# Adding expert results onto the token rows: VectorE sums against accumulating GpSimd transfers

## The chip, the cores and the metric

The kernel runs on one core of a Trainium2 chip. The metric is device time in microseconds. The kernel before takes 485.4 us (median of three runs, 483.75 to 485.8). The profiled execution shown below took 485.2 us, and its span from the first to the last instruction is 483.5 us, so 1.7 us lie outside the span. Times in the rows count from the start of the span.

## What is computed

4096 tokens of width 256 go through a cross-attention block and then through a mixture of eight experts, of which each token uses two.

```python
x = x + cross_attention(layernorm(x), ctx)        # called x1 below
h = layernorm(x)
probs = softmax(h @ gate_w.T); topw, sel = top_k(probs, 2); topw /= topw.sum(-1)
expert_out[e] = (silu(g) * u) @ w2[e].T           # g, u = split(h @ w1[e].T)
out = x + sum over the two chosen experts of topw * expert_out[e]
```

The last line is what the change is about: for each token, two result rows of 256 floats are added to that token's row of x1, and the sum is the output.

## The kernel before

The tokens are 32 tiles of 128 rows. The first part (some 310 us) does the attention tile by tile and keeps x1 for all tiles in SBUF, in the tensor `x1` (printed as `x` in the trace). Each tile's normalised rows are scattered into a table in memory that is sorted by expert.

The second part is a software pipeline over 71 slots of 128 sorted rows. A turn i of `turn2` does a piece of four slots on each engine: SyncE (SP) has loaded slot i, TensorE transposes slot i, multiplies slot i-1 with the first weights, transposes the activations of slot i-2 and multiplies slot i-3 with the second weights. ScalarE (ACT) in turn i does, in this order, `hst_hi(i)`, `silu(i-1)`, `au_hi(i-2)` and `y_copy(i-3)`; VectorE (DVE) does `hst_lo(i)`, `gate_mult(i-1)` and `au_lo(i-2)`. GpSimd (POOL) sends each finished slot with `send_y(slot)`, an indirect transfer that scatters 128 rows of 1 KB into `expert_out`, where a token's two results lie side by side. The slot's result buffer is one of four (`YRING`), so `y_copy(m)` waits for the send of slot m-4. Note the lag: `send_y(s)` follows `y_copy(s)`, and that is part of turn s+3.

Because the first 16 tiles are routed ahead of the rest, their results are complete when slot `DONE` = 39 has been sent; 24, 28, 30 and 32 tiles are complete after 55, 63, 67 and 71 slots.

What is done with the results before the change: for each pair of tiles g (16 of them), SP loads 512 KB of `expert_out` into one of five SBUF buffers (`load_results`), DVE adds the two choices (`add_choices`, line 1320) and then x1 (`add_rows`, line 1325), and ACT issues the store of the pair (`store_results`, line 821). These steps are written into the turns: from turn 48 (`FIN_FIRST`) on, DVE does `add_choices` in one turn and `add_rows` in the next, and ACT issues the store a turn later.

Each engine runs its own instructions strictly in the order in which they are written; a wait stops all that follows it on that engine. The lines that the steps touch:

Of the kernel before, what the change touches and what calls it, by code (L numbers as in the profile page):

```python
# [7 lines left out]
ALU = mybir.AluOpType  # L8
ACT = mybir.ActivationFunctionType
AX = mybir.AxisListType  # L10
F32 = mybir.dt.float32
# [6 lines left out]
P = 128  # L18
B, L, D = 64, 64, 256
# [5 lines left out]
NT = T // P  # L25
# [11 lines left out]
NSLOT = 71  # L37
BOUNDS = (16, 24, 28, 30)
EARLY = BOUNDS[0]
# [55 lines left out]
def build_in(nc, stack, x, ctx_t, w_proj, w_out, w_exp, w_gate, bias, norm_q, norm_k, out,  # L95
             sorted_rows, expert_out):
    def sb(name, shape, dt):
        return stack.enter_context(nc.sbuf_tensor(name, shape, dt))

    def sem(name):  # L100
        return stack.enter_context(nc.semaphore(name))
# [47 lines left out]
    v_bd = sb("v_bd", [P, 2, NB, 2, NPAIR * VW], F32)  # L149

    qp = sb("qp", [P, 2, NQ, 2, KC, NB, L], F16)
# [21 lines left out]
    row = sb("row", [P, 2, SKEW, ROW], F32)  # L173
# [27 lines left out]
    def words(t, pattern):  # L201
        return t.rearrange(pattern)
# [35 lines left out]
    cum2_of = words(square[:, :, :], "p a d -> p (a d)").bitcast(F32)[:, 0:NE * NE].rearrange("p (e f) -> p e f", e=NE)  # L238
    past2_of = past2_of.rearrange("p (a s) -> p a s", a=2)

    def fin_buffers(t, n):
        return [t[:, at * 4 * D:(at + 1) * 4 * D].rearrange("p (m k d) -> p m k d", k=2, m=2) for at in range(n)]

    fin_early = [b for t, n in (
        (words(row[:, :, :, :], "p k s d -> p (k s d)"), 2),
        (qp[:, :, :, :, :, :, :].rearrange("p u g n c b l -> p (u g n c b l)").bitcast(F32), 2),
        (words(v_bd[:, :, :, :, :], "p u b q d -> p (u b q d)"), 1)) for b in fin_buffers(t, n)]
    FIN_BUF = len(fin_early)
    FIN_EARLY = BOUNDS[1] // 2
    FIN_LATE = BOUNDS[-1] // 2  # L250
    assert EARLY_DONE + EARLY >= DONE[1]
    fin_late = [we[:, n * 4 * D:(n + 1) * 4 * D].bitcast(F32).rearrange("p (m k d) -> p m k d", k=2, m=2)
                for we in (we_h, we_l) for n in range(NT // 4)]
    fin_in = (fin_early * 3)[0:FIN_LATE] + fin_late[0:NT // 2 - FIN_LATE]
    FIN_FIRST = EARLY_DONE + 9

    gate_cols = slice(D, DG)
    count_cols = slice(D, D + 3 * NE)
# [43 lines left out]
    y_sent = [sem(f"y_sent{r}") for r in range(4)]  # L302
    names2 = """h2_transposed h2_h_ready h2_l_ready gate_up silu_ready act_ready act_transposed
        au_h_ready au_l_ready y_done y_ready""".split()
    F = {n: sem(n) for n in names2}
    fin_loaded = [sem(f"fin_loaded{n}") for n in range(8)]
    fin_stored = [sem(f"fin_stored{n}") for n in range(FIN_BUF)]
    fin_sum1, fin_sum2 = sem("fin_sum1"), sem("fin_sum2")


    tr_bank = bank[:, 0, :]
# [24 lines left out]
    def _(sp):  # L336
# [97 lines left out]
            load_slot(slot)  # L434
        send_pads()

        ev = expert_out.rearrange("(p t k) d -> p t k d", k=2, p=P)

        def load_results(g):
            if FIN_BUF <= g < FIN_LATE:  # L440
                sp.wait_ge(fin_stored[g % FIN_BUF], 16 * (g // FIN_BUF))
            need(sp, fin_loaded[g % 8], 16 * (g // 8))
            sp.dma_start(fin_in[g], ev[:, 2 * g:2 * g + 2, :, :]).then_inc(fin_loaded[g % 8], 16)

        for slot in range(RING, NSLOT):
            if slot == FULL:
                sp.wait_ge(plan, PLAN)
                sp.wait_ge(pads_sent, 16 * (NE + 1))
                for s in range(SKEW):
                    for k in range(2):  # L450
                        sp.wait_ge(row_sent[k][s], 16 * (NT // SKEW))

            sp.wait_ge(y_sent[slot % YRING], ((slot - RING) // YRING + 1) * 16)
            load_slot(slot)
            g = (slot - EARLY_DONE - RING) // 2
            if (slot - EARLY_DONE - RING) % 2 == 0 and 0 <= g < FIN_EARLY:
                load_results(g)
        for g in range((NSLOT - 1 - EARLY_DONE - RING) // 2 + 1, FIN_EARLY):
            load_results(g)
        for done, low, high in zip(DONE[2:], BOUNDS[1:], BOUNDS[2:] + (NT,)):  # L460
            for r in range(4):
                sp.wait_ge(y_sent[r], 16 * ((done - 1 - r) // YRING + 1))
            for g in range(low // 2, high // 2):
                load_results(g)
        for n in range(FIN_BUF):
            sp.wait_ge(fin_stored[n], 16 * ((NT // 2 - 1 - n) // FIN_BUF + 1))


    @block.gpsimd
    def _(pool):  # L470
        done = [0]
# [147 lines left out]
        for slot in range(NSLOT):  # L619
            send_y(slot // RING, slot % RING)  # L620


    @block.scalar
    def _(act):
# [132 lines left out]
        t = Tile(0, 0)  # L757
# [58 lines left out]

        ov = out.rearrange("(t p) d -> p t d", p=P)

        def store_results(g):
            act.wait_ge(fin_sum2, g + 1)  # L820
            act.dma_start(ov[:, 2 * g:2 * g + 2, :], fin_in[g][:, :, 0, :]).then_inc(fin_stored[g % FIN_BUF], 16)

        for i in range(NSLOT + 3):
            turn2(i // RING, i % RING, True)
            g = (i - FIN_FIRST - 2) // 2
            if (i - FIN_FIRST) % 2 == 0 and 0 <= g < FIN_EARLY:
                store_results(g)
        for g in range((NSLOT - FIN_FIRST) // 2 + 1, NT // 2):
            store_results(g)


    @block.vector
    def _(dve):
        done = [0]
# [325 lines left out]
        for n in range(2):  # L1160
            t = Tile(0, n)
# [153 lines left out]
            if i == 8 + CLASSES:  # L1315
                list_shared()

        def add_choices(g):
            dve.wait_ge(fin_loaded[g % 8], 16 * (g // 8 + 1))
            dve.tensor_tensor(fin_in[g][:, :, 0, :], fin_in[g][:, :, 0, :], fin_in[g][:, :, 1, :], ALU.add  # L1320
                              ).then_inc(fin_sum1, 1)

        def add_rows(g):
            dve.wait_ge(fin_sum1, g + 1)
            dve.tensor_tensor(fin_in[g][:, :, 0, :], fin_in[g][:, :, 0, :], x1[:, 2 * g:2 * g + 2, :], ALU.add
                              ).then_inc(fin_sum2, 1)

        for i in range(NSLOT + 3):
            turn2(i // RING, i % RING, True)
            g = (i - FIN_FIRST) // 2  # L1330
            if 0 <= g < FIN_EARLY:
                if (i - FIN_FIRST) % 2 == 0:
                    add_choices(g)
                else:
                    add_rows(g)
        for g in range(NT // 2):
            if FIN_FIRST + 2 * g > NSLOT + 2 or g >= FIN_EARLY:
                add_choices(g)
            if FIN_FIRST + 2 * g + 1 > NSLOT + 2 or g >= FIN_EARLY:
                add_rows(g)  # L1340


    @block.tensor
# [377 lines left out]
```

## Time and profile before

| what | value |
|---|---|
| median of three runs | 485.4 us |
| profiled execution, and its span | 485.2 us, 483.5 us |
| PE busy, of the span | 438.5 us (91%) |
| DVE busy | 388.1 us (80%) |
| ACT busy | 276.5 us (57%) |
| POOL busy | 308.7 us (64%) |
| TensorE clock granted, mean | 0.984 |

A busy time is an average over parts with different limits: PE is busy for 99% of the turns in the middle of the second part and for 92% of its last 22 turns, where DVE has the extra sums. So the part and its waits are read by stretches. A clock of 1.00 is 2.4 GHz, 0.50 is 1.2 GHz.

### The profile page before, as it was taken

Reading aid. Unit: us, or ns where it says so; the run is one execution under the profiler, and the core shown is the slowest. Engines: PE = TensorE matmul, PEld = TensorE weight load, DVE = VectorE, ACT = ScalarE, POOL = GpSimd, SP = SyncE. Lnnn points to the kernel's source line nnn. Section 1 sums busy time; section 2 is a strip of 40 time slices with the busy share of each in tenths; the row PEclk is TensorE's granted clock in tenths of the full one; section 3 lists DMA queues with packets and bytes.
Section 4 is the critical chain, followed back from the end, with each engine's and each line's share of the span. In section 5 each row is a group of like instructions: output and inputs, shape, how many; then the busy total and the mean of one; then the engine's idle time right before and its main releaser. Section 6 shows DMA issues by size and latency. Waiting matters only on the chain.

```text
span 483.5 us, 15249 instructions
## 1 busy us (share of the span) xinstructions
PE 438.5 (91%) x4428; PEld 383.3 (79%) x4428; DVE 388.1 (80%) x1336; ACT 276.5 (57%) x802; POOL 308.7 (64%) x529
## 2 busy tenths in 40 slices
PE   7898999999999999889999998889999999998980
PEld 3567888878887887778888886679999999898870
DVE  7544888888888898898998978778876767899893
ACT  5353667666665666656666653365566656655650
POOL 6842547887888878777788786576444444444451
PEclk9997999999999999999999999999999999999996
DMA  7253443233232332423333322545444445789964
GB/s 206 82 142 82 140 141 111 87 108 95 81 114 85 104 94 86 118 75 94 104 93 92 105 86 75 148 162 166 133 132 123 127 128 153 240 254 316 309 201 157
DMA packets 55514, 64.62 MB, mean 134 GB/s; under 512 B 9599, under 2 KB 49034, under 8 KB 55434
## 3 DMA queue, kind: packets, MB, share of 16 engines
q1 hardware_dynamic: 44602, 42.59, 31.9%
q0 software_dynamic: 6480, 16.85, 9.8%
q10 hardware_dynamic: 4352, 4.20, 2.5%
q8 instruction: 39, 0.64, 0.6%
q14 instruction: 41, 0.34, 0.2%
HBM read 32.73 MB, written 23.14 MB: 116 GB/s over the span
## 4 chain that ended last, share of the span: by engine, by line
PE 48%; POOL 24%; issue 13%; DVE 12%; ACT 1%; DMA 1%; POOLq 1%; DVEq 0%; ACTq 0%; SPq 0%
PE bank L1351 9%; PE bank L1352 8%; PE bank L1353 8%; POOL sorted_rows L542 7%; PE bank L1592 4%; POOL r_qk L498 3%; POOL we_l L490 3%; POOL ct_l L484 2%; POOL rstd L498 2%; PE bank L1412 2%; PE bank L1625 2%; PE bank L1624 2%; PE bank L1614 2%; PE bank L1613 2%; POOL row L527 1%
## 5 line engine op out<-in xcount | busy, mean ns | idle before, releaser
L614 POOL DMA_INDIRECT expert_out<-probs,late x71 | 72.7, 1024 | 75.1 <-ACT probs L800 70.3
L542 POOL DMA_INDIRECT sorted_rows<-row,place_i x64 | 69.0, 1079 | 33.4 <-POOL row L534 14.8
L1351 PE MATMUL bank<-we_h,xt_h 128*128 x142 | 51.7, 364 | 0.8 <-DVE xt_l L1265 0.8
L705 ACT ACTIVATE probs<-bank 128x1024 f32<-128x1024 f32 x32 | 32.8, 1026 | 23.4 <-PE bank L1465 21.5
L1352 PE MATMUL bank<-we_l,xt_h 128*128 x142 | 45.8, 323 | 0.0
L1353 PE MATMUL bank<-we_h,xt_l 128*128 x142 | 45.7, 322 | 0.0
L788 ACT ACTIVATE xn<-bank 128x176 f32<-128x176 f32 x71 | 22.6, 318 | 37.4 <-PE bank L1353 37.3
L1275 DVE SCALAR_TENSOR_TENSOR probs<-xn,late,bank 128x128 f32<-128x128 f32 x71 | 24.5, 345 | 20.9 <-ACT xn L788 20.2
L932 DVE TENSOR_REDUCE bank<-bank 128x16 f32<-128x1024 f32 x32 | 39.1, 1223 | 2.0 <-PE bank L1400 2.0
L498 POOL TENSOR_TENSOR rstd<-veps,half_neg 128x1 f32<-128x1 f32 x64 | 36.6, 572 | 5.3
L800 ACT COPY probs<-bank 128x256 f32<-128x256 f32 x71 | 26.4, 372 | 18.7 <-PE bank L1625 17.2
L1412 PE MATMUL bank<-v_bd,probs 128*64 128x34 f32 x1024 | 35.3, 225 | 0.2 <-ACT probs L705 0.2
L1465 PE MATMUL bank<-neg_max_t,head_of 128*128 128x128 bf16 x256 | 35.2, 219 | 0.0
L1461 PE MATMUL bank<-qp,late 128*128 128x256 f16 x128 | 34.9, 273 | 0.0
L1463 PE MATMUL bank<-qp,late 128*128 128x256 f16 x128 | 34.9, 273 | 0.0
L1462 PE MATMUL bank<-qp,late 128*128 128x256 f16 x128 | 34.9, 273 | 0.0
L1265 DVE TENSOR_TENSOR xt_l<-bank,xt_h 128x256 fp32r<-128x256 f32 x71 | 30.1, 424 | 5.8 <-ACT xt_h L782 2.5
L1592 PE MATMUL bank<-ident,late 128*128 128x128 f32 x142 | 29.4, 289 | 5.8 <-issue 5.2
L670 ACT COPY neg_max_t<-bank 128x128 bf16<-128x128 bf16 x32 | 8.5, 265 | 45.4 <-PE bank L1441 45.4
L1412 PEld LDWEIGHTS bank<-v_bd,probs 128*64 128x64 f32 x1024 | 33.4, 141 | 0.4 <-ACT probs L705 0.4
L782 ACT CAST xt_h<-bank 128x256 fp32r<-128x256 f32 x71 | 26.6, 375 | 9.6 <-PE bank L1592 7.6
L1359 PE MATMUL bank<-bias_hl,ones_row 128*128 128x264 f32 (+1 forms) x96 | 31.0, 323 | 0.0
(234 smaller groups left out, 1597.0 us busy)
## 6 DMA issues: line engine op xcount, KB each, us to landing
late<-sorted_rows SPq DMA_DIRECT2D x71, 129.0 KB, 2.4
we_f<-w_exp SPq DMA_DIRECT2D x32, 152.0 KB
v_bd<-v_sb SPq DMA_DIRECT2D x128, 34.0 KB
ctx_in<-ctx_t SPq DMA_DIRECT2D x32, 128.0 KB, 2.4
qp<-q_hl SPq DMA_DIRECT2D x128, 32.0 KB
x<-x SPq DMA_DIRECT2D x3, 1024.0 KB, 5.7
row<-expert_out SPq DMA_DIRECT2D x6, 512.0 KB, 5.1
qp<-expert_out SPq DMA_DIRECT2D x6, 512.0 KB, 4.4
```

The costliest lines, as they stand in the source:

```text
L498: pool.tensor_tensor(out_, tmp, half_neg[:, 0:tmp.shape[1]], ALU.pow).then_inc(done_, 1)
L542: pool.indirect_dma_start(sorted_rows, bass.IndirectOffsetOnAxis(ap=place_i[:, t.slot // 2, k, t.par:t.par + 1], axis=0), row[:, k, t.slot ...
L614: pool.indirect_dma_start(expert_out, bass.IndirectOffsetOnAxis(ap=hs(r)[:, D:D + 1].bitcast(U32), axis=0), y_sb[:, r % YRING, :], None, b ...
L932: dve.tensor_reduce(row_max, score_bank.rearrange("p (h k) -> p h k", h=NH), AX.X, ALU.max).then_inc(S["max_found"], 1)
L1351: pe.matmul(dst, a_h, b_h, start=start, stop=False)
L1352: pe.matmul(dst, a_h, b_l, start=False, stop=False)
L1353: return pe.matmul(dst, a_l, b_h, start=False, stop=stop)
L1412: ins = pe.matmul(av_bank[b * L:(b + 1) * L, g * 2 * VW:(g + 1) * 2 * VW], probs[:, t.par, at:at + L], v_bd[:, t.par, b, :, g * VW:(g + 1) ...
L1461: pe.matmul(dst, k_h, q_h, start=True, stop=False)
L1462: pe.matmul(dst, k_h, q_l, start=False, stop=False)
L1465: ins = pe.matmul(dst[:, gh * P:(gh + 1) * P], head_of[:, (b * KC + c) * NQ // 2 + gh, :], neg_max_t[:, t.par, :], start=False, stop=gh == ...
L1592: ins = pe.transpose(bank[:, p, c * P:(c + 1) * P], hs(r)[:, c * P:(c + 1) * P], ident[:, :])
```

## The change

Results of tiles 0 to 29 are no longer loaded, summed by DVE and stored from a buffer. Instead POOL issues transfers that add rows of `expert_out` onto `x1` in SBUF (`accum_op=ALU.add`), for four tiles at a time (a fold), one transfer for the first choice (k = 0) and one for the second (k = 1). The fold's k = 1 waits for the landing of its k = 0. There are seven folds of four tiles and one of two tiles, 16 transfers in all. ACT stores each fold from `x1` (512 KB) when both have landed. Only the last two tiles are loaded by SP and summed by DVE as before, and their store goes out last.

```diff
-    fin_early = [...]            # five SBUF buffers; FIN_EARLY, FIN_FIRST, fin_late and so on go
+    FOLDS = [(low, min(low + 4, high), done) for low, high, done in zip((0,) + BOUNDS, BOUNDS, DONE)
+             for low in range(low, high, 4)]
+    free = 0
+    for f, (low, high, done) in enumerate(FOLDS):
+        at = max(free, done + 2)
+        ADDS.setdefault(at, []).append((f, 0))
+        ADDS.setdefault(at + 2, []).append((f, 1))
+        STORES.setdefault(min(at + 6, NSLOT + 2), []).append(f)
+        free = at + 1
...
+    def results_done(eng, done):
+        for r in range(YRING):
+            eng.wait_ge(y_sent[r], 16 * ((done - 1 - r) // YRING + 1))
...
-            if (slot - EARLY_DONE - RING) % 2 == 0 and 0 <= g < FIN_EARLY:
-                load_results(g)          # SP; and the later loads of the same kind
+        results_done(sp, NSLOT)
+        sp.dma_start(fin_in, ev[:, LAST_TILES, :, :]).then_inc(fin_loaded, 16)
+        sp.wait_ge(fin_stored, 16 * (len(FOLDS) + 1))
...
+        def add_results(f, k):           # POOL
+            low, high, done = FOLDS[f]
+            if k == 0:
+                results_done(pool, done)
+            else:
+                pool.wait_ge(fold_added[f], 16)
+            pool.dma_start(x1[:, low:high, :], ev[:, low:high, k, :], accum_op=ALU.add).then_inc(fold_added[f], 16)
+        for slot in range(NSLOT + 3):
+            if slot < NSLOT:
+                send_y(slot // RING, slot % RING)
+            for f, k in ADDS.get(slot, ()):
+                add_results(f, k)
...
-            act.wait_ge(fin_sum2, g + 1) # ACT, a pair of tiles
+        def store_results(f):            # ACT, a fold
+            low, high, done = FOLDS[f]
+            act.wait_ge(fold_added[f], 32)
+            act.dma_start(ov[:, low:high, :], x1[:, low:high, :]).then_inc(fin_stored, 16)
         for i in range(NSLOT + 3):
             turn2(i // RING, i % RING, True)
+            for f in STORES.get(i, ()):
+                store_results(f)
+        act.wait_ge(fin_sum2, 1)
+        act.dma_start(ov[:, LAST_TILES, :], fin_in[:, :, 0, :]).then_inc(fin_stored, 16)
...
-                    add_choices(g)       # DVE, inside the turns: 16 pairs
-                    add_rows(g)
+        dve.wait_ge(fin_loaded, 16)      # DVE, after the last turn: one pair
+        dve.tensor_tensor(fin_in[:, :, 0, :], fin_in[:, :, 0, :], fin_in[:, :, 1, :], ALU.add).then_inc(fin_sum1, 1)
+        dve.wait_ge(fin_sum1, 1)
+        dve.tensor_tensor(fin_in[:, :, 0, :], fin_in[:, :, 0, :], x1[:, LAST_TILES, :], ALU.add).then_inc(fin_sum2, 1)
```

The schedule that these rules give: the transfers of fold f stand on POOL behind `send_y` of the slots 41, 42, 43, 44 (k = 0) and 43, 44, 45, 46 (k = 1) for folds 0 to 3; 57, 58 and 59, 60 for folds 4 and 5; 65 and 67 for fold 6; 69 and 71 for fold 7. The stores stand on ACT at the end of turns 47, 48, 49, 50, then 63, 64, 71 and 73.

POOL before, the end of its program: the last scatter transfers of the first part, then the sends of all slots in one run (`expert_out<-probs`; each row gives the operation and what it waits for).

```order
L529 TENSOR_TENSOR row<-e_gap,row 128x2 [waits weight_set2]
L534 COPY row<-result_row 128x2 [waits row2_ready]
L542 DMA sorted_rows<-row,place_i 33920x258 [waits weight_set3,place_set,ids_set] x2
L534 COPY row<-result_row 128x2 [waits row2_ready]
L542 DMA sorted_rows<-row,place_i 33920x258 [waits weight_set3,place_set,ids_set] x2
L614 DMA expert_out<-probs,late 8192x256 [waits y_ready] x71
L90 UNCONDITIONAL_BRANCH
```

Nothing stood between two sends.

POOL now, from the sends of slots 0 to 41 on (`x<-expert_out` is a fold's transfer onto x1; line numbers are those of the changed kernel).

```order
L602 DMA expert_out<-probs,late 8192x256 [waits y_ready] x42
L614 DMA x<-expert_out 128x4x256 [waits y_sent2,y_sent3,y_sent1,y_sent0]
L602 DMA expert_out<-probs,late 8192x256 [waits y_ready]
L614 DMA x<-expert_out 128x4x256 [waits y_sent2,y_sent3,y_sent1,y_sent0]
L602 DMA expert_out<-probs,late 8192x256 [waits y_ready]
L614 DMA x<-expert_out 128x4x256 [waits fold_added0]
L614 DMA x<-expert_out 128x4x256 [waits y_sent2,y_sent3,y_sent1,y_sent0]
L602 DMA expert_out<-probs,late 8192x256 [waits y_ready]
L614 DMA x<-expert_out 128x4x256 [waits fold_added1]
```

Between the sends stand now the transfers that add; the one that waits for `fold_added0` (fold 0, k = 1) comes two sends behind that fold's first, and the sends of slots 44 and later stand behind it.

ACT before, around the first store: the four operations of turns 50 and 51 and the store of the first pair of tiles.

```order
L788 ACTIVATE xn<-bank 128x176 [waits act_ready,gate_up]
L793 CAST at_h<-bank 128x256 [waits y_done,act_transposed]
L800 COPY probs<-bank 128x256 [waits y_sent3,y_done]
L821 DMA out<-row 128x2x256 [waits fin_sum2]
L782 CAST xt_h<-bank 128x256 [waits gate_up,h2_transposed]
L788 ACTIVATE xn<-bank 128x176 [waits act_ready,gate_up]
```

This store, the first of 16, has moved three turns ahead and carries four tiles.

ACT now, turns 47 and 48 with the stores of folds 0 and 1 (L801 is `y_copy`, of slots 44 and 45 here).

```order
L794 CAST at_h<-bank 128x256 [waits y_done,act_transposed]
L801 COPY probs<-bank 128x256 [waits y_sent0,y_done]
L823 DMA out<-x 128x4x256 [waits fold_added0]
L783 CAST xt_h<-bank 128x256 [waits gate_up,h2_transposed]
L789 ACTIVATE xn<-bank 128x176 [waits act_ready,gate_up]
L794 CAST at_h<-bank 128x256 [waits y_done,act_transposed]
L801 COPY probs<-bank 128x256 [waits y_sent1,y_done]
L823 DMA out<-x 128x4x256 [waits fold_added1]
```

A store waited for a sum of DVE (`fin_sum2`) and waits now for both transfers of its fold (`fold_added`); behind it stands, as before, the next turn's `hst_hi`.

## Rows read from the trace of the kernel before

**Rows 1.** Busy time by engine over the span, from the page
```profile
PE 438.5 (91%) x4428; PEld 383.3 (79%) x4428; DVE 388.1 (80%) x1336; ACT 276.5 (57%) x802; POOL 308.7 (64%) x529
```

**Rows 2.** Busy time in stretches: turns 14 to 47, turns 48 to 69, the rest
```profile
core 0: us, PE busy (x) PEld busy (x) DVE busy (x) ACT busy (x) POOL busy (x), PEclk, DMA share, GB/s
344.12:414.40 70.28, 69.83 (x510) 67.26 (x509) 50.71 (x170) 42.98 (x136) 32.75 (x34) 1.00 0.45 132
414.40:465.44 51.04, 47.08 (x331) 43.68 (x331) 46.86 (x133) 29.44 (x88) 24.78 (x23) 1.00 0.88 284
465.44:483.50 18.06, 5.25 (x36) 4.36 (x34) 9.89 (x21) 3.04 (x9) 5.17 (x5) 0.76 0.49 152
```

**Rows 3.** Timeline of DVE, one turn with a sum: start, us, engine, line, operation
```profile
442.33 0.42 DVE L1265 TENSOR_TENSOR xt_l<-bank,xt_h 128x256 fp32r<-128x256 f32 x1
...
443.77 0.69 DVE L1320 TENSOR_TENSOR row<-row 128x512 f32<-128x512 f32 x1
444.50 0.42 DVE L1265 TENSOR_TENSOR xt_l<-bank,xt_h 128x256 fp32r<-128x256 f32 x1
```

**Rows 4.** Chain that ended last, its end: start us, us, what
```profile
467.46 0.69 DVE row L1320
...
473.22 2.63 DMA expert_out<-probs,late
475.98 3.46 DMA we_h<-expert_out
479.46 0.70 DVE we_h L1320
480.19 0.69 DVE we_h L1325
```

**Rows 5.** Timeline of ACT: y_copy of slots 43 and 44
```profile
411.61 0.37 ACT L800 COPY probs<-bank 128x256 f32<-128x256 f32 x1 [0.22 <-PE bank L1625]
...
413.72 0.37 ACT L800 COPY probs<-bank 128x256 f32<-128x256 f32 x1 [0.22 <-PE bank L1625]
```

**Rows 6.** Timeline of POOL: the sends of slots 41, 42 and 43
```profile
408.69 0.97 POOL L614 DMA_INDIRECT expert_out<-probs,late  x1 [1.03 <-ACT probs L800]
410.76 0.97 POOL L614 DMA_INDIRECT expert_out<-probs,late  x1 [1.10 <-ACT probs L800]
412.75 0.97 POOL L614 DMA_INDIRECT expert_out<-probs,late  x1 [1.02 <-ACT probs L800]
```

**Rows 7.** Timeline of DVE and PE: hst_lo of slot 45, and what uses it
```profile
408.23 0.42 DVE L1265 TENSOR_TENSOR xt_l<-bank,xt_h 128x256 fp32r<-128x256 f32 x1
...
409.55 0.41 PE L1351 MATMUL bank<-we_h,xt_h 128*128 x1
```

**Rows 8.** Line 443, SP's loads of 512 KB of results: issue, us to landing
```profile
L443 SPq DMA_DIRECT2D row<-expert_out x6: 332/436/458, 408.2 to 452.6; - x6
...
DMA to landing us min/median/max: 3.5/4.6/6.8
```

**Rows 9.** Line 821, ACT's stores of 256 KB: us to landing
```profile
DMA to landing us min/median/max: 2.1/3.9/6.8
```

**Rows 10.** POOL's own DMA queue: packets, MB, share of 16 engines' span
```profile
q0 software_dynamic: 6480, 16.85, 9.8%
```

**Rows 11.** Timeline of PE around an idle time in the first part
```profile
35.72 0.38 PE L1368 MATMUL bank<-ident,xn 128*128 128x128 f32 x2
38.41 1.06 PE L1400 MATMUL bank<-late,qp 128*64 128x128 f16 x16 [2.32 <-issue]
```

**Rows 12.** Busy time by microsecond there; the eighth number is the clock
```profile
36.00:37.00 1.00, 0.10 (x1) 0.00 (x0) 0.47 (x1) 1.00 (x3) 0.70 (x1) 1.00 1.09 307
37.00:38.00 1.00, 0.00 (x0) 0.00 (x0) 0.56 (x2) 0.27 (x1) 0.00 (x0) 0.93 0.70 205
...
43.00:44.00 1.00, 1.00 (x4) 0.81 (x3) 0.47 (x2) 0.00 (x0) 0.00 (x0) 0.50 0.09 26
44.00:45.00 1.00, 1.00 (x6) 0.48 (x6) 0.00 (x0) 0.12 (x1) 0.00 (x0) 0.66 0.15 40
```

More of the change, by code:

```diff
@@ L239, in build_in @@
     past2_of = past2_of.rearrange("p (a s) -> p a s", a=2)
[L241 to L255, printed above, removed]
+    FOLDS = [(low, min(low + 4, high), done) for low, high, done in zip((0,) + BOUNDS, BOUNDS, DONE)
+             for low in range(low, high, 4)]
+    LAST_TILES = slice(BOUNDS[-1], NT)
+    fin_in = words(row[:, :, :, :], "p k s d -> p (k s d)")[:, 0:4 * D].rearrange("p (m k d) -> p m k d", k=2, m=2)
+    assert NT - BOUNDS[-1] == 2
+    ADDS = {}
+    STORES = {}
+    free = 0
[5 more added lines that the diff above has]
+        free = at + 1
     gate_cols = slice(D, DG)
@@ L305, in build_in @@
     F = {n: sem(n) for n in names2}
-    fin_loaded = [sem(f"fin_loaded{n}") for n in range(8)]
-    fin_stored = [sem(f"fin_stored{n}") for n in range(FIN_BUF)]
+    fold_added = [sem(f"fold_added{f}") for f in range(len(FOLDS))]
+    fin_loaded, fin_stored = sem("fin_loaded"), sem("fin_stored")
     fin_sum1, fin_sum2 = sem("fin_sum1"), sem("fin_sum2")
+    ev = expert_out.rearrange("(p t k) d -> p t k d", k=2, p=P)
+    def results_done(eng, done):
+        for r in range(YRING):
+            eng.wait_ge(y_sent[r], 16 * ((done - 1 - r) // YRING + 1))
     tr_bank = bank[:, 0, :]
@@ L435, in _ @@
         send_pads()
[L437 to L443, printed above, removed]
         for slot in range(RING, NSLOT):
@@ L454, in _ @@
             load_slot(slot)
-            g = (slot - EARLY_DONE - RING) // 2
-            if (slot - EARLY_DONE - RING) % 2 == 0 and 0 <= g < FIN_EARLY:
-                load_results(g)
[L458 to L466, printed above, removed]
+        results_done(sp, NSLOT)
+        sp.dma_start(fin_in, ev[:, LAST_TILES, :, :]).then_inc(fin_loaded, 16)
+        sp.wait_ge(fin_stored, 16 * (len(FOLDS) + 1))
     @block.gpsimd
@@ L617, in send_y @@
             ).then_inc(y_sent[r % YRING], 16)
-        for slot in range(NSLOT):
-            send_y(slot // RING, slot % RING)
+        def add_results(f, k):
[10 more added lines that the diff above has]
+                add_results(f, k)
+        assert max(ADDS) < NSLOT + 3
     @block.scalar
@@ L1316, in turn2 @@
                 list_shared()
[L1318 to L1326, printed above, removed]
         for i in range(NSLOT + 3):
             turn2(i // RING, i % RING, True)
-            g = (i - FIN_FIRST) // 2
-            if 0 <= g < FIN_EARLY:
-                if (i - FIN_FIRST) % 2 == 0:
-                    add_choices(g)
-                else:
-                    add_rows(g)
[L1336 to L1340, printed above, removed]
+        dve.wait_ge(fin_loaded, 16)
+        dve.tensor_tensor(fin_in[:, :, 0, :], fin_in[:, :, 0, :], fin_in[:, :, 1, :], ALU.add).then_inc(fin_sum1, 1)
+        dve.wait_ge(fin_sum1, 1)
+        dve.tensor_tensor(fin_in[:, :, 0, :], fin_in[:, :, 0, :], x1[:, LAST_TILES, :], ALU.add).then_inc(fin_sum2, 1)
     @block.tensor
```

7 lines of the change are left out of this document (removed).

## The prediction

> **What bounds the kernel now.** I read the busy times first, then the stretches of the second part, then timelines of single turns, then the end of the chain. PE is busy for 91% of the span [rows 1], and in the turns without sums it sets the pace: turns 14 to 47 take 70.28 us, of which PE works 69.83, so a turn is 70.28 / 34 = 2.07 us; DVE needs 50.71 / 34 = 1.49 us of it [rows 2]. From turn 48 on, DVE does a sum of 0.69 us in each turn: 1.49 + 0.69 = 2.18, and a turn with a sum starts 2.17 us after the one before it [rows 3]. DVE is the limit there: 51.04 us for 22 turns, 46.86 of them DVE's [rows 2]. After the last send the chain is serial: landing 2.63 us, load 3.46, two sums 0.70 and 0.69, and then the last store to the end of the span, 483.5 - 480.9 = 2.6 us [rows 4].
>
> **What is removed.** With no sums, turns 48 to 69 fall back to PE's pace: 51.04 - 22 x 2.07 = 5.5 us. One more sum stands on the chain in the tail, 0.69 us [rows 4]. Together -6.2 us. SP's 15 loads and ACT's smaller stores are off the chain and I count them at nothing; the same bytes move in the new transfers.
>
> **What is added: a wait on ACT.** The point is the order. Fold 0's k = 1 stands on POOL behind the send of slot 43. Its store stands on ACT at the end of turn 47, and turn 47 ends with the copy of slot 44, because a copy is three turns behind its slot's number. In today's times: the copy of slot 43 ends at 411.61 + 0.37 = 411.98 [rows 5]; the send starts 0.77 later and takes 0.97, so POOL is free at 413.72 [rows 6]; ACT ends the copy of slot 44 at 414.09 [rows 5]. So ACT waits for a transfer that starts at most 0.37 us before. All of turn 48 on ACT is queued behind it: `hst_hi(48)`, which PE's first multiplication of slot 48 needs. PE has slack: `hst_lo` ends at 408.65 and the multiplication that needs it starts at 409.55 [rows 7], 0.9 us.
>
> **The price of a transfer, L, from its start on POOL to its landing.** No row shows an accumulating transfer, so bounds. Below: the last send, 128 rows, lands after 2.63 us [rows 4]; a plain load of the same 512 KB needs 3.5 at the fastest [rows 8]. Above: a fold has 512 rows of 1 KB, a send 128; if POOL's 0.97 us [rows 6] grew with the rows it were 3.9 us, and with the median plain load behind it L = 3.9 + 4.6 = 8.5. I take the nearest row: the median plain load of 4.6 us [rows 8], with POOL's 0.97 for issuing in place of SP's 0.44 [rows 8]: L = 5.1.
>
> The rule that speaks for a short L: the Trainium skill, "DMA: Bandwidth & Descriptors", section "Anatomy of one DMA — SWDGE (gpsimd) path", says that generating descriptors is a small part of a transfer and that many can be emitted before it shows. No row here has two sizes of POOL transfer, so the trace neither confirms nor denies it; by it POOL's share would stay near 0.97, which is the value taken: 506 us in the sum below, against 545 with the 3.9.
>
> **The sum with L = 5.1.** Fold 0's k = 0 starts behind the send of slot 41, at 408.69 + 0.97 = 409.66 [rows 6], and lands at 414.76; its k = 1 waits for that and lands at 419.86. ACT stands from 414.09 to 419.86, 5.8 us. Then ACT needs about 1.7 us for its issue and the turn's four operations, whose inputs are ready. Followed on in this way (POOL: 0.97 for each transfer and each send, in the order of its program), the stores are released at 419.9, 422.8, 428.3 and 431.3; without waits the fourth would be due at 414.09 + 3 x 2.06 = 420.3. That is 11.0 us, less PE's slack of 0.9: **10.1 us** for folds 0 to 3. Folds 4 and 5 are the same as 0 and 1, and POOL has less to do between them: 5.8 + 0.2 - 0.9 = **5.1 us**. Fold 6's store stands on ACT between the copies of slots 68 and 69, another 5.8 us on the way to the last send; there fold 7's k = 0 also stands on POOL before the last send (0.97 us). With some of it running beside the short last turns, the end comes **5.3 us** later; fold 7's own two transfers and store end at about the same time as the last pair's.
>
> **The clock.** After its matmul of 35.72 PE does nothing until 38.41 [rows 11]. The granted clock falls from 1.00 (2.4 GHz) at the end of this idle time and is 0.50 (1.2 GHz) until some 44.3 [rows 12], 6.5 us, while PE is at work from 38.41 on. Half of 6.5 us is lost: 3.2 us. The stops of folds 0 and 4 (and 2) leave PE idle for longer than those 2.3 us. Part of the slow time falls into the smaller waits that follow, so I count one drop for each of the two groups of folds: **6.4 us**. In the tail little PE work is left.
>
> Sum: -6.2 + 10.1 + 5.1 + 5.3 + 6.4 = +20.7. Against the profiled execution's own 485.2 us that is 505.9: **506 us**. The profiled execution is 0.2 below the median of 485.4, so no correction.
>
> **Ends.** The same walk with L = 3.5 gives 5.9 + 2.2 + 2.7 and between no and two clock drops: 490 to 496. With L = 2.63 it is 4.1 + 1.4 + 1.9 and no drop (PE stands 1.4 us): 486. With L = 8.5, 3.9 of it on POOL, the sends stand behind the descriptors too: 29.2 + 15.8 + 14.3 + 6.4 - 6.2 = +59.5: 545.
>
> **Rivals.**
>
> *Two reads for each row.* An adding transfer reads the row in memory and the row of x1, so the 16 engines might need twice the time for it. POOL's queue moved 16.85 MB in 9.8% of 16 x 483.5 us [rows 10], 45 us of one engine for each MB; another 0.52 MB over 16 engines is 1.5 us. L = 6.6 gives 14.7 + 7.9 + 8.3 + 6.4 - 6.2 = +31: 516 us. For it: the engines are busy for 0.88 of turns 48 to 69 already [rows 2], so the extra work cannot hide. Against it: the waits themselves thin out the other traffic. The Trainium skill states such a rule for collectives ("Collectives: The Full Stack", section "The bandwidth ceiling: the fold count and why AG ≠ RS ≠ AR"): a reduction runs at about half the rate of a gather because it reads two sources for each chunk. No run here shows it yet.
>
> *POOL becomes the bound.* If descriptors cost by the row, eight transfers of 3.9 us and six sends stand in six turns; time 525 to 545. Against it: a part of the send's 0.97 is surely fixed.
>
> *The transfer is quick.* L of 2.6 to 3.9 gives 486 to 498.
>
> *The other side: faster.* The stores' wait is hidden, as it is now. Then the sums' 6.2 us come back, less about 1 us for fold 7's transfer before the last send: 480 us. It needs the second transfer to land within 0.37 + 0.9 = 1.3 us of its start; above that each fold's store costs PE time, and at L of about 2.5 the gain is used up. The shortest landing of any result transfer is 2.1 us, a plain 256 KB store at the end, beside nothing else [rows 9].
>
> **Chances.** Forecast (500 to 511): 0.43. Two reads (511 to 525): 0.25. POOL the bound: 0.12. Quick: 0.15, of which 0.05 within 0.5% of before. Faster: 0.05. Half a per cent, 2.4 us, is about what a measurement of this kernel can tell from no change. So faster 0.05, same 0.05, slower 0.90. The range reaches from the quick case's 490 to 528, just into the case of POOL; what is left out is most of that case, the faster one and the quickest transfers, 0.2 together.
>
> **What the profile will show.** Right: ACT's longest waits are the stores of folds 0, 2, 4 and 6, about 5 to 6 us each, released by the adding transfers; PE idle beside them, granted clock 0.50 behind the stops; DVE turns without a sum at 1.5 us of work; POOL rows of about 1 us for 512 rows. Wrong: adding rows of 3 us and more on POOL (the case of POOL); landings above 6 us behind short POOL rows (two reads); no wait of ACT at the stores, with turns of 2.07 us to the end (faster). If ACT's waits are there but PE's turns do not stretch, the slack of 0.9 us was read too small.

## The result, and the profile after

The changed kernel takes 522.6 us (median of four runs, 521.9 to 522.8) against 484.8 us for the kernel before in the same session (four runs, 483.8 to 485.8): ratio 1.0785, 95% interval 1.0761 to 1.0808. It is 37.9 us slower; the forecast was about 21 us slower, 506 us, with a range of 490 to 528. The profiled execution took 522.4 us, its span is 520.6 us. Lines of the kernel after differ from those before by a few: `y_copy` is L801, `hst_hi` L783, `hst_lo` L1266, `send_y` L602, the adding transfers L614, a fold's store L823.

The page's busy times [rows 1] say that PE works 7 us longer for the same 4428 multiplications, and DVE 20 us less.

```profile
PE 445.6 (86%) x4428; PEld 390.5 (75%) x4428; DVE 368.1 (71%) x1306; ACT 274.9 (53%) x802; POOL 328.3 (63%) x545
```

By stretches (columns as in [rows 2]): turns 14 to 47, the first group of folds, quiet turns, the second group, and the rest.

```profile
343.29:411.55 68.26, 67.80 (x495) 65.11 (x493) 49.21 (x165) 41.88 (x132) 33.17 (x34) 1.00 0.43 125
411.55:453.00 41.45, 26.10 (x142) 23.49 (x142) 13.49 (x46) 11.17 (x38) 19.08 (x18) 0.75 0.99 215
453.00:465.21 12.21, 11.87 (x86) 11.19 (x85) 8.54 (x29) 7.60 (x24) 6.90 (x7) 1.00 0.45 132
465.21:492.69 27.48, 19.40 (x122) 18.32 (x121) 11.76 (x41) 10.04 (x32) 12.94 (x13) 0.81 0.74 156
492.69:520.60 27.91, 5.84 (x36) 4.88 (x34) 4.53 (x13) 2.94 (x9) 10.02 (x9) 0.66 0.57 115
```

Up to 411.55 nothing has changed. In the first group PE works for 26 of 41 us while the 16 DMA engines are busy for 0.99 of the time; in the quiet turns between the groups PE is again at work all the time.

Who holds PE is in the waits of ACT from 405 us on (engine, line waited at, releaser: us in all, times, longest):

```profile
ACT xt_h L783 <- DMA x<-expert_out: 34.2, 5, 9.3
...
ACT at_h L794 <- DMA x<-expert_out: 8.6, 1, 8.6
```

The six waits are the stores of folds 0, 1, 2, 4, 5 and 6 (the profile books a wait for a store at the next operation, `hst_hi`, and at `au_hi` in the tail). They are 42.8 us in all, and PE stands beside them: in the two groups DVE waits for ACT's `hst_hi`, and PE for DVE.

```profile
DVE xt_l L1266 <- ACT xt_h L783: 37.7, 12, 9.5
...
PE bank L1335 <- DVE xt_l L1266: 19.0, 4, 6.9
```

How much of the loss hangs on the place of these waits, and how much on the transfers, is for the experiments. One of the waits in ACT's timeline (start, us, operation, idle ahead of it), against [rows 5]: the copy of slot 44, the store, and the next turn's first operation.

```profile
412.88 0.37 ACT L801 COPY probs<-bank 128x256 f32<-128x256 f32 x1 [0.23 <-PE bank L1609]
422.02 0.42 ACTq L823 DMA_DIRECT2D out<-x  x1
422.54 0.37 ACT L783 CAST xt_h<-bank 128x256 fp32r<-128x256 f32 x1 [9.29 <-DMA x<-expert_out]
```

The transfers themselves, L614 on POOL: ns of one (min/median/max), and from issue to landing.

```profile
L614 POOL DMA_DIRECT2D x<-expert_out x16: 1242/1388/1885, 408.9 to 512.2; - x16
...
DMA to landing us min/median/max: 4.6/6.8/13.2
```

So POOL needs 1.39 us for 512 rows where a send of 128 took 0.97 [rows 6], and the landing is 6.8 us in the median where the plain loads of 512 KB had 4.6 [rows 8]. (Fold 7's two transfers are of 256 KB, and the 4.6 is one of them.) POOL's timeline in the first group shows the transfers one behind the other:

```profile
415.31 2.67 POOL L614 DMA_DIRECT2D x<-expert_out  x2 [0.80 <-DMA expert_out<-probs,late]
...
425.54 1.35 POOL L614 DMA_DIRECT2D x<-expert_out  x1
...
433.59 1.30 POOL L614 DMA_DIRECT2D x<-expert_out  x1 [1.15 <-DMA x<-expert_out]
```

The first `x2` is fold 0's second transfer and fold 2's first; the next send starts behind both.

What the clock did beside it, in stretches of 2 us (the eighth number), with PE's busy time and the DMA share:

```profile
416.00:418.00 2.00, 1.00 (x6) 0.81 (x7) 0.00 (x0) 0.00 (x0) 1.98 (x2) 1.00 1.21 232
418.00:420.00 2.00, 0.29 (x2) 0.05 (x1) 0.00 (x0) 0.00 (x0) 1.72 (x2) 0.97 1.18 205
420.00:422.00 2.00, 0.00 (x0) 0.00 (x0) 0.00 (x0) 0.00 (x0) 2.00 (x2) 0.50 1.21 224
...
430.00:432.00 2.00, 1.60 (x5) 1.61 (x6) 1.24 (x5) 0.56 (x3) 0.64 (x1) 0.50 1.20 245
432.00:434.00 2.00, 2.00 (x11) 1.77 (x10) 0.00 (x0) 0.00 (x0) 0.85 (x2) 0.62 1.17 246
434.00:436.00 2.00, 0.07 (x1) 0.00 (x0) 0.00 (x0) 0.00 (x0) 0.90 (x1) 1.00 1.17 238
436.00:438.00 2.00, 0.00 (x0) 0.00 (x0) 0.00 (x0) 0.00 (x0) 0.00 (x0) 0.73 1.16 286
```

The clock falls to 0.50 (1.2 GHz) once PE has stood, as in [rows 12], and stays there until 433; when PE stands again, at 434, it falls a second time in the same group. A DMA share above 1 means that the records of packets overlap, so a share counts the time that packets take, and what they wait for may be in it. In these windows the engines move 205 to 286 GB/s, over the whole first group 215; before, turns 48 to 69 had a share of 0.88 and 284 GB/s [rows 2]. More of the packets' time, and less moved: that is new.

The chain's end, against [rows 4]: fold 6's second transfer, its store on ACT, the last copies, and then the same serial end as before with a 0.61 us piece of fold 7's transfer ahead of the last send.

```profile
498.29 6.03 DMA x<-expert_out
504.34 0.38 ACTq L823
...
507.25 0.61 POOL x L614
507.87 1.04 issue
508.90 3.04 DMA expert_out<-probs,late
512.09 3.57 DMA row<-expert_out
```

Where the 37 us of span are, from the starts of `hst_lo` on DVE (the experiments below are in the same table; times in us):

| kernel | turns 47 to 56 | 57 to 62 | 63 to 69 | turn 70 to the end |
|---|---|---|---|---|
| before | 22.9 | 14.2 | 16.0 | 18.1 |
| after | 42.7 | 13.0 | 25.4 | 27.9 |
| late stores | 32.7 | 13.4 | 17.3 | 25.7 |
| plain copies | 37.6 | 13.0 | 21.0 | 22.0 |
| both | 25.5 | 13.4 | 14.5 | 22.7 |
| 4 KB stretches | 43.4 | 12.9 | 24.5 | 27.9 |
| late, 4 KB, spread | 25.4 | 16.0 | 17.6 | 24.2 |

After less before: +19.8, -1.2, +9.4 and +9.8, and the first part ended 0.8 us earlier; together +37.

### The profile page after: what moved, and what is told of

It reads as the page before. It is cut to its first block, busy times and chain, and to the rows that moved or that the text cites. A ratio compares the mean times of both kernels' runs of the same rounds, so it can differ in the third digit from the quotient of the medians.

```text
span 520.6 us, 15216 instructions
## 1 busy us (share of the span) xinstructions
PE 445.6 (86%) x4428; PEld 390.5 (75%) x4428; DVE 368.1 (71%) x1306; ACT 274.9 (53%) x802; POOL 328.3 (63%) x545
## 4 chain that ended last, share of the span: by engine, by line
PE 39%; POOL 25%; issue 14%; DVE 10%; DMA 9%; ACT 2%; POOLq 1%; ACTq 0%; DVEq 0%; SPq 0%
PE bank L1335 8%; PE bank L1336 7%; PE bank L1337 7%; POOL sorted_rows L530 7%; DMA x<-expert_out 6%; POOL r_qk L486 3%; PE bank L1576 3%; POOL we_l L478 3%; POOL ct_l L472 2%; POOL rstd L486 2%; DMA expert_out<-probs,late 2%; POOL expert_out L602 2%; PE bank L1396 1%; POOL row L515 1%; PE bank L1609 1%
## 5 line engine op out<-in xcount | busy, mean ns | idle before, releaser
L602 POOL DMA_INDIRECT expert_out<-probs,late x71 | 70.4, 992 | 88.0 <-ACT probs L801 79.8
L1335 PE MATMUL bank<-we_h,xt_h 128*128 x142 | 54.5, 384 | 19.9 <-DVE xt_l L1266 19.9
L1266 DVE TENSOR_TENSOR xt_l<-bank,xt_h 128x256 fp32r<-128x256 f32 x71 | 30.1, 425 | 43.5 <-ACT xt_h L783 40.3
L783 ACT CAST xt_h<-bank 128x256 fp32r<-128x256 f32 x71 | 26.6, 375 | 40.5 <-DMA x<-expert_out 34.2
L1336 PE MATMUL bank<-we_l,xt_h 128*128 x142 | 47.9, 337 | 0.0
L1337 PE MATMUL bank<-we_h,xt_l 128*128 x142 | 47.8, 336 | 0.0
L1335 PEld LDWEIGHTS bank<-we_h,xt_h 128*128 128x128 f32 x142 | 28.5, 201 | 21.7 <-issue 21.7
L1276 DVE SCALAR_TENSOR_TENSOR probs<-xn,late,bank 128x128 f32<-128x128 f32 x71 | 24.6, 346 | 28.0 <-ACT xn L789 27.9
L789 ACT ACTIVATE xn<-bank 128x176 f32<-128x176 f32 x71 | 22.6, 318 | 37.9 <-PE bank L1337 37.3
L801 ACT COPY probs<-bank 128x256 f32<-128x256 f32 x71 | 26.6, 374 | 17.6 <-PE bank L1609 17.5
L1335 PE MATMUL bank<-we_h,at_h 128*128 x71 | 27.2, 383 | 10.0 <-DVE at_h L1289 8.7
L1576 PE MATMUL bank<-ident,late 128*128 128x128 f32 x142 | 30.3, 296 | 4.9 <-issue 4.7
```

What stands on the lines that cost most here:

```text
L602: pool.indirect_dma_start(expert_out, bass.IndirectOffsetOnAxis(ap=hs(r)[:, D:D + 1].bitcast(U32), axis=0), y_sb[:, r % YRING, :], None, b ...
L1335: pe.matmul(dst, a_h, b_h, start=start, stop=False)
L1336: pe.matmul(dst, a_h, b_l, start=False, stop=False)
L1337: return pe.matmul(dst, a_l, b_h, start=False, stop=stop)
L1576: ins = pe.transpose(bank[:, p, c * P:(c + 1) * P], hs(r)[:, c * P:(c + 1) * P], ident[:, :])
```

## The experiments

Two theories. The first: what costs is where the store's wait stands, on ACT in front of the next turn. The second: what costs is the transfer, because the addition makes the DMA engines do each byte twice. Both had their part in the forecast; the runs were to say how much each has, and whether the forecast's other terms hold.

**Stores six turns later.**

```diff
-        STORES.setdefault(min(at + 6, NSLOT + 2), []).append(f)
+        STORES.setdefault(min(at + 12, NSLOT + 2), []).append(f)
```

> The changed kernel, with each fold's store put six turns later on ScalarE (12 turns behind the fold's first transfer, not 6). Nothing is left out. Theory 1 (the place of the wait costs the time: ScalarE stands at the store, and its next turn with it): nearly all of the loss of the two groups of folds goes, PE stays at some 2.06 us a turn, and the time is about 482 us (before's 484.8, less 5.5 for the sums in turns 48 to 69, plus some 3 in the tail). Theory 2 (the 16 DMA engines are full: an adding transfer needs some 2.3 times the engine time of a send, and eight of them in a row, 4.2 MB, fill all 16 engines for some 27 us, during which the loads of the slots, the sends and the waits on GpSimd stand too): the wait only moves from ScalarE to GpSimd's queue and to the slots' data, the first group of folds still costs some 10 us, and the time is about 495 to 500 us. Under both, the landings stay as in the changed kernel (median near 6.8 us), longest near 12 us.

Measured: 501.2 us, ratio to before 1.0347 (1.0296 to 1.0399). 21.4 us of the 37.9 went, not all. ACT no longer waits for the adds. POOL does, with the sends behind it, and PE's longest waits stand now ahead of the first transposition of a turn (L1576). The waits from 400 to 480 us, and the stretch from turn 40 to the end:

```profile
PEld bank L1576 <- issue: 12.4, 16, 1.8
POOL x L614 <- DMA x<-expert_out: 10.6, 4, 4.3
```

```profile
395.36:498.80 103.44, 71.28 (x486) 65.47 (x484) 49.06 (x163) 41.78 (x129) 57.19 (x51) 0.90 0.85 192
```

The time is just above the 495 to 500 us of the second theory. The landings stay, as both said (6.9 us in the median, 12.1 the longest).

**Plain copies in place of the addition.**

```diff
-            pool.dma_start(x1[:, low:high, :], ev[:, low:high, k, :], accum_op=ALU.add).then_inc(fold_added[f], 16)
+            pool.dma_start(x1[:, low:high, :], ev[:, low:high, k, :]).then_inc(fold_added[f], 16)
```

> The changed kernel, with plain copies in place of the adding transfers: same bytes, same rows, same waits and queue, without the accumulation (the sum of the result rows is left out). Theory 2 (an adding transfer moves each row twice through the DMA engines): the engine time of GpSimd's queue for the eight folds falls from some 105 us for each MB to some 45, landings fall from a median of 6.8 us to 4.6 to 5.1, and the time to about 506 us, what the forecast's sum gives with a transfer of 5.1 us. Rival (512 rows of 1 KB from GpSimd's queue are slow as such, and the accumulation is free): landings stay near 6.8 us and the time near 522 us.

Measured: 504.9 us, ratio 1.0414 (1.0353 to 1.0474). The transfers of this kernel (L614), and the stretch from turn 40 to the end:

```profile
L614 POOL DMA_DIRECT2D x<-expert_out x16: 755/808/851, 407.7 to 495.9; - x16
...
DMA to landing us min/median/max: 3.1/5.2/8.4
```

```profile
396.11:503.90 107.79, 74.84 (x486) 70.55 (x484) 48.78 (x163) 40.74 (x129) 47.26 (x51) 0.84 0.58 184
```

The same stretch of before and of after:

```profile
398.08:483.50 85.42, 68.65 (x486) 63.99 (x484) 68.68 (x193) 42.54 (x129) 37.72 (x35) 0.95 0.73 232
```

```profile
397.28:520.60 123.32, 77.48 (x486) 71.80 (x484) 48.75 (x163) 40.57 (x129) 57.13 (x51) 0.80 0.72 161
```

Time by DMA share is the work of all 16 engines: 85.42 x 0.73 = 62.4 us before, 107.79 x 0.58 = 62.5 with copies, 123.32 x 0.72 = 88.8 with the addition. The addition alone adds 26 us of all 16 engines. POOL's queue in this stretch (packets, MB, share), before, with copies and with the addition:

```profile
q0 software_dynamic: 1728, 3.81, 12.1%
```

```profile
q0 software_dynamic: 3904, 11.67, 32.9%
```

```profile
q0 software_dynamic: 9664, 11.67, 50.2%
```

Less the sends' 0.121 x 85.42 = 10.3 us, taken as the same in all three, the 11.67 - 3.81 = 7.86 MB of result rows need 0.329 x 107.79 - 10.3 = 25.2 us as copies (51 us of one engine for each MB) and 0.502 x 123.32 - 10.3 = 51.6 us as additions (105 us): 2.05 times as much. (These are sums of the packets' time.) So the size of the second theory's price is shown; that it is a second pass over each byte is only its reading, since no record shows the pass itself. One thing moves with it: the 7.86 MB go in packets of 4 KB as copies and of 1 KB as additions (3904 against 9664 packets). The next run takes that apart.

The two transfers of fold 6 stand apart from the others, in the tail. They landed after 5.9 and 6.0 us in the changed kernel, and after 3.9 us each as copies.

**Results in stretches of 4 KB.**

```diff
-    ev = expert_out.rearrange("(p t k) d -> p t k d", k=2, p=P)
+    ev = expert_out.rearrange("(p k t) d -> p t k d", k=2, p=P)
...
-        setup(pool.iota(result_row[:, :, :], [[1, 2], [2, NT]], base=0, channel_multiplier=2 * NT))
+        setup(pool.iota(result_row[:, :, :], [[NT, 2], [1, NT]], base=0, channel_multiplier=2 * NT))
```

> The changed kernel, with the results laid out in memory so that a fold's four tiles of one choice are one stretch of 4 KB for each partition in place of four of 1 KB (another table of result rows, and the last load in two pieces). Nothing is left out. Theory 2, cost by the byte (each byte is read twice): the engine time for each MB stays near 105 us, and so do the landings (6 to 7 us); the time is 515 to 522 us. Rival, cost by the descriptor (each 1 KB row pays a fixed price twice): engine time for each MB falls to half or less, landings to some 4 us, the rows of the adding transfers on GpSimd get shorter than 1.39 us, and the time is about 500 us or less.

Measured: 519.5 us, ratio 1.0734 (1.0671 to 1.0798). Its transfers (L615 there), and POOL's queue from turn 40 to the end:

```profile
L615 POOL DMA_DIRECT2D x<-expert_out x16: 883/954/1203, 406.3 to 508.4; - x16
...
DMA to landing us min/median/max: 4.2/7.1/12.5
```

```profile
q0 software_dynamic: 4032, 11.67, 44.5%
```

```profile
394.77:517.80 123.03, 79.58 (x486) 73.59 (x484) 48.69 (x163) 40.48 (x129) 50.31 (x51) 0.77 0.66 161
```

Packets are nearly as few as with copies (4032), and POOL's time for one transfer falls from 1.39 to 0.95 us; but the landing stays at 7.1 us and the time falls by 3 us only, to where the second theory put it. The result rows need 0.445 x 123.03 - 10.3 = 44.4 us, 90 us of one engine for each MB: neither the 105 that this theory expected nor the half that the rival did. Of the 26.4 us that the addition adds, 7.2 go with the smaller packets and 19.2 stay. So most of the price goes by the byte: with packets of 4 KB on both sides an addition takes 1.77 times what a copy takes, and costs 519.5 - 504.9 = 14.6 us.

**The sums on VectorE cut, in the kernel before.** This is the term that the forecast put at 6.2 us.

```diff
-            dve.tensor_tensor(fin_in[g][:, :, 0, :], fin_in[g][:, :, 0, :], fin_in[g][:, :, 1, :], ALU.add
+            c = slice(0, D if g == NT // 2 - 1 else 1)
+            dve.tensor_tensor(fin_in[g][:, :, 0, c], fin_in[g][:, :, 0, c], fin_in[g][:, :, 1, c], ALU.add
...   (the sum with x1 in the same way)
```

> The kernel before, with the sums on VectorE cut to one column of 256 for all but the last pair of tiles, so that every load, wait, store and instruction count is as before and only the time of the sums goes (the sums are left out). It measures the term that the forecast put at 5.5 + 0.7 = 6.2 us. If VectorE is what holds turns 48 to 69, as the forecast reads it, turns fall from 2.17 to 2.07 us and the time to about 479 us. Rival (the full DMA engines or PE hold those turns, and VectorE only beside them): the time falls by under 2 us, to 483 to 484 us.

Measured: 483.5 us, ratio 0.9982 (0.9956 to 1.0008): the rival. That is 0.4 us, which can't be told from nothing. Turns 48 to 69 of this kernel:

```profile
414.74:465.98 51.24, 47.18 (x332) 43.70 (x331) 36.41 (x133) 29.53 (x88) 21.70 (x23) 1.00 0.87 276
```

DVE has 10 us less work than in [rows 2] and the stretch takes as long. What PE waits for there stands in the waits of the kernel before, turns 48 to 69, in which PE has no row that ends at DVE:

```profile
PEld bank L1592 <- issue: 6.4, 13, 1.1
```

L1592 is the transposition of the slot's rows, the first of a turn; in turns 14 to 47 the same row has 1.2 us in 4 waits. "issue" means that no wait that the profile sees explains it.

**Late stores and plain copies together** (the edits of the first two runs).

> Late stores and plain copies together: the changed kernel with each store six turns later on ScalarE and without the accumulation (the sum of the result rows is left out). Theory 2 (with ScalarE freed, what is left of the loss is the second pass of each added byte through the DMA engines): from turn 40 to the end the engines' work falls from 88 us of all 16 to 62 us, the same as in the kernel before, PE keeps its 2.06 us a turn outside a few us, and the time is 480 to 488 us. Rival (what late stores alone left, 17 us, is GpSimd's queue with its waits and its sends behind them, whatever the transfers do): the time stays above 495 us.

Measured: 487.6 us, ratio 1.0079 (1.0049 to 1.0108). The stretch from turn 40 to the end, and ACT's only wait for a transfer from 405 us on:

```profile
396.40:486.70 90.30, 69.06 (x486) 64.13 (x484) 48.97 (x163) 41.13 (x129) 47.20 (x51) 0.93 0.69 219
```

```profile
ACT probs L801 <- DMA expert_out<-probs,late: 6.6, 4, 2.4
```

The engines' work is 90.30 x 0.69 = 62.3 us, as before. PE's waits ahead of the transposition (L1576), 12.4 us with late stores alone, are 3.1 us here. With the four kernels the loss is divided: the addition costs 522.6 - 504.9 = 17.7 us where ACT waits and 501.2 - 487.6 = 13.6 where it doesn't; the place of the wait costs 21.4 us with additions and 504.9 - 487.6 = 17.3 with copies; 3.7 us are left with neither. The table has 4.6 us more in the tail, where the last fold's transfer still stands ahead of the last send, and 2.6 more in turns 47 to 56, where four of ACT's `y_copy` waited for sends that stood behind transfers on POOL; turns 57 to 69 and the first part give some back.

**Less traffic, in the kernel before.** Loads and stores of one partition, sums whole; and then with the sums cut too.

```diff
-            sp.dma_start(fin_in[g], ev[:, 2 * g:2 * g + 2, :, :]).then_inc(fin_loaded[g % 8], 16)
+            p = slice(0, P if g == NT // 2 - 1 else 1)
+            sp.dma_start(fin_in[g][p], ev[p, 2 * g:2 * g + 2, :, :]).then_inc(fin_loaded[g % 8], 16)
...   (the store in the same way)
```

> The kernel before, with its loads of results and stores of the output cut to one of 128 partitions for all but the last pair of tiles (so most of the output is left out), and VectorE's sums whole. Cutting the sums alone changed turns 48 to 69 by nothing (2.33 us a turn in both). If the DMA traffic in these turns makes PE's waits before its transpositions, and VectorE is a second limit of 2.17 us just under it: turns fall from 2.33 to 2.17 to 2.2 us, the time by 3 to 4 us to about 481. Rival (the traffic has no part in it): no change, 484 us.

> The kernel before, with both cut: loads and stores to one partition, and VectorE's sums to one column, for all but the last pair (most of the output is left out). If the two limits, sums and traffic, stand beside each other in turns 48 to 69, only taking both away brings PE back to 2.06 us a turn: 22 turns x (2.33 - 2.06) = 6 us, the time about 478 to 479 us. Rival (something else in these turns holds PE, such as the longer path of the last slots): under 3 us, 482 us or more.

Measured: 481.4 us, ratio 0.9925 (0.9895 to 0.9955), and 479.5 us, ratio 0.9890 (0.9866 to 0.9914). Turns 48 to 69 of the one and of the other:

```profile
414.75:463.77 49.02, 48.29 (x338) 44.51 (x337) 46.27 (x132) 29.30 (x89) 27.10 (x23) 1.00 0.34 104
```

```profile
414.12:460.97 46.85, 46.35 (x332) 43.80 (x332) 36.32 (x133) 28.63 (x88) 21.39 (x22) 1.00 0.36 108
```

By 22 turns: 2.32 us a turn before, 2.33 without sums, 2.23 without traffic, 2.13 without either. Both times are near what was expected (481, and 478 to 479), the turns a little above (2.2 and 2.06). Two limits stand side by side: taking the sums away alone gives nothing, taking the traffic away leaves the sums to hold the turns. The two intervals just overlap; it is the turns that tell the two kernels apart. With less traffic PE's waits ahead of the transposition fall from 6.4 to 2.7 us.

**The register load of PE, in the kernel before.**

```diff
-                found[r] = weights_of(i - 1)
+                if i == 1:
+                    found[r] = weights_of(0)
...
                 gate_up(i - 1, (r - 1) % 2, found[r])
+                if i < NSLOT:
+                    found[(r + 1) % RING] = weights_of(i)
```

> The kernel before, with PE's read of the weight offset of a slot (a register load from SBUF that stands ahead of each turn's first transposition) moved behind the gate and up multiplications of the turn ahead. Nothing is left out. PE's waits in front of that transposition sum to 6.4 us in turns 48 to 69 and 1.2 us in turns 14 to 47. If they are the register load, late while the DMA engines are busy, and the six multiplications ahead of its new place hide it: turns go to VectorE's 2.17 us, the time falls by 2 to 4 us, to about 481. Rival (they wait for something else, or the load stalls PE's queue just as long at its new place): no change or slower, 484 to 486 us.

Measured: 481.4 us, ratio 0.9921 (0.9891 to 0.9950). It is 2.6 us faster than the kernel before. Turns 48 to 69:

```profile
413.52:463.47 49.95, 48.88 (x338) 43.99 (x338) 46.20 (x133) 29.65 (x90) 25.80 (x23) 1.00 0.89 281
```

PE's waits ahead of the transposition are gone from its waits there (3.4 us stand elsewhere, 1.2 of them ahead of the transposition of the activations, which now comes behind the read), and most turns are at DVE's 2.17 us. Of the gain 51.04 - 49.95 = 1.1 us lie in these turns; some 1.5 us come from turns 14 to 47, at 2.02 us a turn in place of 2.07. The read of the weight offset was what PE waited for: the slot's load, for which the same transposition waits too, was not moved. Why the read is late beside busy DMA engines no run here shows.

**The best form of the change, and the same with the early offsets.** On top of the 4 KB stretches:

```diff
-        ADDS.setdefault(at + 2, []).append((f, 1))
-        STORES.setdefault(min(at + 6, NSLOT + 2), []).append(f)
-        free = at + 1
+        ADDS.setdefault(at + 3, []).append((f, 1))
+        STORES.setdefault(min(at + 10, NSLOT + 2), []).append(f)
+        free = at + 4
```

> The change in the form that the first runs point to: stores four turns of GpSimd behind the second transfer of their fold, results in stretches of 4 KB, and a fold's transfers spread out (a fold every four turns, its second transfer three turns behind the first). Nothing is left out. Theory 2 (the engines' work, 81 us of all 16 from turn 40 to the end, against 62 before and 88 in the changed kernel, sets the floor; the order decides how much of it lies beside PE's work): with the work spread from turn 41 on, 488 to 496 us, better than late stores alone (501) but still slower than before. Rival (only the waits cost, the engines' work is hidden once no engine waits for a landing): 480 to 484 us.

> The best form of the change so far (late stores, 4 KB stretches, transfers spread out; 494 us) with PE's read of a slot's weight offset behind the gate and up multiplications, which alone brought the kernel before to 481 us. Nothing is left out. If PE's waits ahead of its first transposition (10.7 us from turn 43 to 70) are that read, held up while the DMA engines are busy, as they were in the kernel before, most of them go: 486 to 490 us, still not below before with the same edit. Rival (with the engines' work as the floor, PE waits elsewhere for the same time): 492 to 495 us.

Measured: 494.1 us, ratio 1.0221 (1.0183 to 1.0259), and 493.4 us, ratio 1.0193 (1.0159 to 1.0227). The stretch from turn 40 to the end of the first:

```profile
395.98:493.40 97.42, 70.27 (x486) 64.15 (x484) 49.06 (x163) 41.63 (x129) 50.66 (x51) 0.93 0.84 203
```

97.42 x 0.84 = 82 us of engine work, as with 4 KB stretches alone: spreading moves the work and doesn't lessen it. The early offsets, worth 2.6 us in the kernel before, gave 0.8 us here, where the intervals overlap: here the rival held. The reason is in PE's waits from turn 43 to 70, without and with the early offsets:

```profile
PEld bank L1577 <- issue: 10.7, 16, 1.8
```

```profile
PEld bank L1598 <- issue: 8.4, 15, 1.1
```

L1577 is the transposition of the slot's rows; L1598 is that of the activations, the first operation behind the read at its new place. The wait moved with the read, and six multiplications didn't hide it. With the addition no form that was tried comes to the time before.

## Why the prediction was right or wrong

The kernel is slower, as forecast, and 522.6 us lies within the range, but the sum was 17 us short.

*The wait on ACT* was read rightly: the stores of folds 0, 2, 4 and 6 stop ACT and PE stands beside them, and that of fold 1 with them (5.8 us). "About 5 to 6 us each" was too little: those four are 9.3, 7.9, 9.3 and 8.6 us. For fold 2 it was also not what the forecast's own walk gives (428.3 - 422.8 - 1.7 = 3.8).

*The price L* is the step that was mis-sized. The forecast took 5.1 us from the plain load's landing and POOL's 0.97. Measured from issue to landing: 6.8 us in the median, 13.2 at the longest, 6.0 for fold 6 in the tail. Of the two parts POOL's was nearly right (1.39, not 0.97, and far from 3.9); the landing was not. With copies, whose transfers land after 5.2 us, the kernel took 504.9 us, and the forecast's sum for 5.1 us was 505.9. So the walk along the queues was good, in total, for the transfer that it assumed. Part of that is luck, since its errors cancel: with copies turns 47 to 56 lost 37.6 - 20.6 = 17.0 us (forecast 13.3, as below), turns 63 to 69 lost 6.6 (8.3), and the tail grew by 3.9 (4.6). What the addition adds is what it left to a rival.

*Two reads for each row* was that rival (chance 0.25, 511 to 525 us, 516 with L = 6.6), and its price and its sign came: landings above 6 us behind short POOL rows, and 2.05 times the engine time of copies, 1.77 times with packets of the same size. The Trainium skill's rule in "Collectives: The Full Stack", section "The bandwidth ceiling: the fold count and why AG ≠ RS ≠ AR", that a reduction with two sources runs at about half the rate of a gather, agrees with these two numbers, though no collective runs here. The time came out some 6 us above the rival's sum. L is no constant, as the sum has it: in the first group fold 0's first transfer landed after 6.1 us, fold 3's after 13.2, with the engines' share at 0.99, and each fold's second transfer waits for its first. That this is the 6 us is likely, but no run takes it apart.

*POOL as the bound* is refuted: 1.39 us for 512 rows, 0.95 for 128 stretches of 4 KB. That 384 more pieces cost 0.44 us agrees with what the Trainium skill says in "DMA: Bandwidth & Descriptors", section "Anatomy of one DMA — SWDGE (gpsimd) path".

*The quick transfer* and *faster* needed landings of 2.6 to 3.9 us and of 1.3 us; the quickest of 512 KB took 5.9.

*What is removed*, -5.5 us for turns 48 to 69, was reasoned wrongly. DVE's busy share of 0.92 and its 2.17 us turns looked like the limit, but cutting the sums alone gave 0.4 us, since PE's late register loads held the turns as well. In the changed kernel both causes left together, sums and traffic: between the groups, in turns 53 to 59, a turn is 2.04 us. So the size of the term nearly held (51.04 - 46.85 = 4.2 us with both cut), by luck. The waits of PE in that stretch would have shown it.

*The groups and the clock.* Against PE's pace of 2.06 us, turns 47 to 56 lost 42.7 - 20.6 = 22.1 us (forecast 10.1 + 3.2 = 13.3), turns 63 to 69 lost 25.4 - 14.4 = 11.0 (5.1 + 3.2 = 8.3). The clock's share can be read apart: from turn 40 to the end PE's busy time is 77.48 us after and 68.65 before, 8.8 us more for the same 486 instructions; forecast 6.4. The forecast counted one drop for each group, and the first group had two. It also read one drop a little short: the last row of [rows 12], 0.66, puts the rise at 44.7, not 44.3. With copies PE's busy time is 6.2 us more, with late stores and copies 0.4.

*The tail* grew by 9.8 us, forecast 5.3 - 0.7 = 4.6: fold 6's store waited 8.6 us instead of 5.8, and its two transfers took 5.9 and 6.0 us, one behind the other. With copies it grew by 3.9.

Where the missing 17 us are, then: by place 22.1 - 13.3 = 8.8 in the first group, 2.7 in the second and 9.8 - 4.6 = 5.2 in the tail; by cause, taking the addition away gives back 17.7 us with ACT's wait left where it is, of which 14.6 stay with packets of 4 KB.

## What to carry to other kernels

Price a transfer that adds at 1.8 to 2 times the engine time of a copy, as measured here, and compare the engines' whole work in the stretch (time by DMA share) with the time that the stretch has, before walking the queues: the plain loads' 4.6 us, taken at a share of 0.88 and less, did not hold for eight adding transfers in a row. A busy share near 0.9 doesn't make an engine the limit: look at who waits for it, and expect a second limit right behind the first. Keep the wait for a landing off an in-order engine that feeds the bound, or put it well behind the earliest landing: six turns, some 12 us, gave back 21 us here.

## What the runs showed of the hardware that was not expected

- The adding transfer from GpSimd took 105 us of one DMA engine for each MB in rows of 1 KB and 90 in rows of 4 KB, against 51 as a copy. With rows of 4 KB in place of 1 KB POOL's own time fell by a third and the landing not at all (7.1 against 6.8 us).
- While such transfers filled the engines, in the first group, they moved 215 GB/s at a share of 0.99; before, 284 GB/s at 0.88.
- PE's read of a register from SBUF at the head of a turn made it wait 6.4 us in 22 turns at a DMA share of 0.88, and 1.2 us in 34 turns at 0.45. The share isn't all of it: with most of the traffic cut the 22 turns still had 2.7 us at 0.34. Moved behind six multiplications, it made the whole kernel before 0.8% faster (0.5 to 1.1). In the spread form of the change the wait went with it to its new place, 8.4 us there against 10.7, and the gain was 0.8 us, within the noise.
